# VectorE takes the next group's gathered rows inside the quad it builds before, in a graph kernel with one step per 1024 edges

## The reference, cut to what matters

```python
def _L0_gnn_ref(node_features, edge_index, edge_features, W1, b1, W2, b2, U1, c1, U2, c2):
    src_features = node_features[src]
    msg_input = jnp.concatenate([src_features, edge_features], axis=-1)
    h = jax.nn.relu(msg_input @ W1 + b1)
    messages = h @ W2 + b2
    aggregated = jax.ops.segment_sum(messages, dst, num_segments=N)
    g = jax.nn.relu(jnp.concatenate([node_features, aggregated], axis=-1) @ U1 + c1)
    return g @ U2 + c2
...
h = jnp.maximum(_layernorm(x), 0.0)
x = x + _L0_gnn_ref(h, edge_index, edge_attr_64, ...)
h = jnp.maximum(_layernorm(x), 0.0)
x = x + segment_sum(h[src] * edge_weight[:, None], dst)
```

## Time and profile before

| | |
|---|---|
| median of 3 runs | 3135.02 us (3133.75 to 3136.86) |
| the profiled execution, its own time | 3122.63 us |
| its span | 3120.8 us |
| TensorE busy | 2232.2 us, 72% |
| VectorE busy | 1629.2 us, 52% |
| GpSimd busy | 1560.8 us, 50% |
| ScalarE busy | 849.5 us, 27% |
| mean granted TensorE clock | 0.812 of full |

### The profile page before, as it was taken

One profiled execution on the slowest core, in us unless ns is written; L12 is line 12 of the kernel. 1 busy time (PEld: TensorE's weight loads), 2 busy tenths in 40 slices (PEclk: granted clock), 3 DMA queues, 4 the chain that ended last, 5 costly groups with the idle time before them and its releaser, 6 DMA issues.

```text
span 3120.8 us, 49909 instructions
## 1 busy us (share of the span) xinstructions
PE 2232.2 (72%) x18336; PEld 1691.8 (54%) x18336; DVE 1629.2 (52%) x4964; ACT 849.5 (27%) x1500; POOL 1560.8 (50%) x1635
## 2 busy tenths in 40 slices
PE   4475755666666677677777777777777777777799
PEld 4354544444444455555555555555555655665577
DVE  4445755555555555555554555545555455554455
ACT  4122433222222222222222222223222322222221
POOL 4635255555555545555555455555555544554400
PEclk9867877777777777777777877888888889888899
DMA  4123444433543454355435543553555356525688
GB/s 89 34 91 133 167 135 154 156 129 121 178 137 118 131 186 149 93 167 166 138 108 164 169 132 119 162 170 114 166 166 154 102 160 181 176 78 155 177 275 289
DMA packets 376799, 459.49 MB, mean 147 GB/s; under 512 B 78474, under 2 KB 298890, under 8 KB 372968
## 3 DMA queue, kind: packets, MB, share of 16 engines
q1 hardware_dynamic: 317914, 401.54, 39.4%
q0 software_dynamic: 51712, 53.06, 7.8%
q10 hardware_dynamic: 6926, 1.63, 0.2%
HBM read 281.50 MB, written 174.54 MB: 146 GB/s over the span
## 4 chain that ended last, share of the span: by engine, by line
PE 51%; issue 16%; another core or an unknown queue 15%; DVE 13%; DMA 2%; ACT 1%; SPq 1%; DVEq 0%; ACTq 0%
PE pair L1303 17%; PE pair L1318 9%; PE pair L1342 7%; PE pair L1243 5%; DVE bld L1818 4%; DVE bld L1828 4%; PE pair L1290 3%; PE pair L1349 2%; PE pair L1236 2%; PE pair L1446 1%; DVE rings L1772 1%; PE pair L1376 1%; DMA late_piece<-adjacency 1%; DVE bld L1821 1%
## 5 line engine op out<-in xcount | busy, mean ns | idle before, releaser
L835 POOL DMA_INDIRECT rows<-table,idx x1464 | 1402.6, 958 | 1245.6 <-DVE rings L1772 851.5
L1009 ACT COPY stage<-pair 128x600 f32<-128x600 f32 x808 | 527.8, 666 | 1760.0 <-remote 767.0
L1818 DVE TENSOR_SCALAR bld<-iota_key,key 128x300 bf16<-128x300 f16 x1616 | 536.8, 332 | 798.8 <-remote 509.7
L1303 PE MATMUL pair<-bld 128*128 128x300 bf16 x4848 | 839.1, 328 | 91.8 <-issue 54.1
L1303 PEld LDWEIGHTS pair<-bld 128*128 128x128 bf16 x4848 | 566.1, 122 | 322.3 <-issue 160.4
L1318 PE MATMUL pair<-stage,h 125*64 125x96 f32 x4230 | 380.0, 310 | 191.2 <-issue 188.8
L1828 DVE TENSOR_TENSOR bld<-bld,part 128x512 bf16<-128x512 bf16 x1212 | 490.7, 405 | 0.0
L1318 PEld LDWEIGHTS pair<-stage,h 125*64 125x64 f32 x4230 | 301.6, 179 | 241.5 <-issue 240.8
L1243 PE MATMUL pair<-w1b,rings 128*128 128x128 f32 x1584 | 264.4, 321 | 164.5 <-DVE rings L1772 160.8
L1243 PEld LDWEIGHTS pair<-w1b,rings 128*128 128x128 f32 x1584 | 244.5, 233 | 185.3 <-DVE rings L1772 176.5
L1342 PE MATMUL pair<-late_piece,h 125*64 125x384 f32 (+1 forms) x1040 | 266.5, 642 | 92.9 <-issue 76.8
(11 more groups left out here) (178 smaller groups left out, 1439.1 us busy)
## 6 DMA issues: line engine op xcount, KB each, us to landing
late_piece<-adjacency SPq DMA_DIRECT2D x232, 480.0 KB
rings<-in_edge_attr_dram SPq DMA_DIRECT2D x202, 256.0 KB
adjacency<-stage SPq DMA_DIRECT2D x14, 2160.0 KB
tail<-stage SPq DMA_DIRECT2D x101, 240.0 KB
stage<-tail SPq DMA_DIRECT2D x50, 480.0 KB, 5.9
rows<-table,idx POOLq DMA_INDIRECT x1464
adjacency<-stage SPq DMA_DIRECT2D x10, 1920.0 KB
adjacency<-stage SPq DMA_DIRECT2D x10, 1680.0 KB
```

Source lines behind the costliest of these rows:

```text
L835: pool.indirect_dma_start(out=to[:, t, :], out_offset=None, in_=table, in_offset=bass.IndirectOffsetOnAxis(ap=idx[:, g, t:t + 1], axis=0), ...
L1009: act.copy(tiles[:, g % STAGE, :, 2 * j * WT:2 * (j + 1) * WT].rearrange("p h (o w) -> p o h w", w=WT), build_pair[i % 2][:, :, 0:KEYS].re ...
L1303: last = pe.matmul(build_pair[i // 2 % 2][:, t % 2, 0:KEYS], hot_w[q % 2][k][:, :, u], hot_key[q % 2][:, u, :], start=(k == 0), stop=(k == ...
L1818: return dve.tensor_scalar(hot_key[q % 2][:, u, :], iota_key[:, :], key[:, g, t + u:t + u + 1], None, ALU.is_equal)
```

## The change

For groups 4 and on, `add_fast(s + 1)` is moved from step s + 1 into step s, behind the first key of quad 2s + 2. It gets a wait for the group's edge terms (`q_made`). Groups 0 to 3 stay where they were.

```diff
                 if g >= RAW:
                     gathered_wait(dve, g, g % RING, 0)
-                else:
-                    dve.wait_ge(q_made, g + 1)
+                dve.wait_ge(q_made, g + 1)
                 of = q_bank.rearrange("p (t f) -> p t f", f=D)
...
-            def make_quad(q):
+            def make_quad(q, take=None):
...
                     if k == 0:
+                        if take is not None:
+                            add_fast(take)
                         dve.wait_ge(eq_made, q + 1)
...
                         add_sums(s - 1)
+                    if s < RAW:
+                        add_fast(s)
                     if s < GROUPS:
-                        add_fast(s)
                         make_hot(s)
...
-                            make_quad(q)
+                            make_quad(q, s + 1 if q % 2 == 0 and s + 1 >= RAW else None)
```

## The result

The changed kernel takes 3296.51 us (median of 4 runs, 3288.36 to 3303.15), the kernel before 3134.39 on the same chip (4 runs, 3128.57 to 3136.86). The ratio is 1.0519, 95% interval [1.0491, 1.0547]: 162 us slower, where 100 us less was forecast. The time lies outside the range and on the other side.

A forecast was written before the change was run, and what follows sets the result against it. The bound was taken to be the loop from add through gather burst and release to the next add. Gains of 16 + 62 + 22 = 100 us turn 3122.6 into 3022.6, plus 12.4 for the median: 3035 us, range 2965 to 3180.

The forecast's parts named there:

- the loop: What sets a step with gathers: add, burst 0.96 us later, release about 11.5 later, then VectorE's remaining work before the next add.
- release: Moment when PE's held-up signals reach VectorE and ACT again; taken as fixed, about 11.5 us after the burst of gathers begins.
- two late products: 78 steps: 1.34 us between release and add in place of 2.3; gain 0.8 each, 62 us; steps of 13.9.
- no late product: 97 steps, 79 with gathers: 0 to 0.33 us between release and add for 0.44; gain 0.2 each, 16 us; steps of 12.8.
- It fits, with nothing to spare: PE's late products, tiles 0 to 3 and `make_q` end 12.0 to 13.0 us after the add, against a release at 12.5.
- the stop: Point in a burst from which PE's signals no longer arrive, some 6.5 us after the add; VectorE was to finish its quads before.
- so PE can run them during the burst: Tiles 0 to 3 and `make_q` no longer wait for their own step's add; PE runs them under the gathers, signalled at the release.
- PE becomes the bound: Rival, slower, chance 0.10: PE's chain stretches by 2 us, the 100 steps with late products lose 0.5 each; 3169 us.
- Bursts run together: Rival: POOL's next burst follows without pause, signals stay away; 3242 or 3098 us. Chance 0.14 everywhere, 0.08 in part of the steps.
- PE's wait is the true cost: Rival, faster, chance 0.06: all 160.8 us of PE's edge-term product waiting for the add go; 2974 us.
- The signs named for a wrong forecast: Gathers without pause and steps alternating near 7 and 21 us; or PE idle for microseconds ahead of L1342, L1807 or a load.
- The rule weighed: VectorE and GpSimd exclude each other on a shared port pair; bursts inside a quad up to 2.3 us longer a step; taken as nothing.

The follow-up runs named there:

- e6: Kernel after with the add moved to the step's end, behind both quads and just ahead of the accumulator's add: 3243.10 us, ratio 1.0337 to the kernel before.
- e14: Kernel after with each batch's direct products cut to the first 10 blocks, the others left out: 3062.76 us, ratio 0.9915 to the kernel before.
- e9: Kernel before with only 4 of a group's 8 gathers issued from group 22 on, half the rows left out: 2161.34 us, ratio 0.7001.
- e12: Kernel before with the add in the early place for groups 4 to 104 alone: 3055.89 us against 3084.42, ratio 0.9906.
- e13: Kernel before with each batch's direct products cut to the first 10 blocks, the others left out: 3097.74 us against 3087.66, ratio 1.0027.
- e7: Kernel after with PE's `make_q` put ahead of tiles 0 to 3: 3359.17 us, ratio 1.071 to the kernel before.
- e8: Kernel after with `make_q` one group earlier on PE, ahead of direct and late products: 3366.97 us, ratio 1.0737 to the kernel before.
- e1: Kernel before with the new wait for `q_made` on all groups, the add left in place: 2232.49 us against 2233.34, ratio 1.0002.
- e11: Kernel after, unchanged, repeated on another chip: 3217.90 us against 3084.42 for the kernel before, ratio 1.043.

## Why the prediction was wrong

**Right: the loop.** Add, burst 0.96 later, release some 11.5 later, rest of VectorE's work, add. It held in the kernel after (11.65), in e6 (11.41) and in e14 (11.64), and e9 shows that the gathers make it. e6 gave all steps one length, as the loop says.

**Right in the first half, in part by luck: two late products.** Forecast 13.9, median 13.80. e12, with the change there alone, is 29 us faster. The 28 steps sum to 9.5 us less, 0.34 each where 0.8 was taken. The forecast had only the release set this step. But PE's chain came out equally long, 7.4 + 6.5 = 13.9, and in 23 of the 28 steps the add follows the end of `make_q` within 0.25 us.

**Nearly right in the first half: no late product.** 12.8 was forecast for 13.01; the medians are 12.93 against 13.06, and 12.77 in e14 against 12.92 in e13. That is 0.13 and 0.15, where 0.2 was taken. The 53 steps sum to 4.6 us less, and the 22 behind group 104 to 19.7 more, so the term of 16 us came out as a loss of 15.

**The step that failed is "It fits, with nothing to spare".** The prediction had `late` start "5 to 6 us after the add's start", and from there 7.5 us for late products, tiles 0 to 3 and `make_q`: "13.0 after the add at the most, 12.0 at the least, against a release at 0.96 + 11.5 = 12.5". With two late products behind group 104 the chain took 8.3 + 7.9 = 16.2 us on average, with three 12.4 + 6.1 = 18.5. It went wrong in three ways.

- *`late` starts later.* With two late products it starts 7.4 us after the add (1176.56, 2021.61), not 5 to 6: VectorE is there after 5.0 (1175.94 - 1.88 = 1174.06) and is then held for 1.9. With three it is held to 11.2 us after the add, and the message sum ends 3.8 us after it on PE instead of 2.5 (medians). The prediction let VectorE and its signals through until the stop, and had the stop come behind the accumulator's add.
- *The direct products were left out.* They stand on PE between the message sum and `late`. They were no part of any path before, because there they ran last in the held-up stretch, with nothing waiting. There are 14 in the step at 1169, 30 in that at 2014 and 40 in that at 2664. With 14 they cost nothing: PE was idle for 4.18 us behind them. With 30 they end at 2020.83 + 0.32 = 2021.15, hardly before the accumulator's add, and with 40 they end 13.4 us after the add (median). e13 and e14 show that their length costs the kernel before nothing and decides the kernel after: without most of them 8.3 + 7.9 becomes 7.0 + 6.0.
- *The row runs in the slow part of the burst.* In the step at 2014 four, three and then one matmul of the late products come with gaps of 0.46 to 0.60 us that no wait explains, and PE ends them at 2026.64. In the step with three late products it is the direct products that trickle:

```profile
2663.95 0.69 DVE L1771 TENSOR_TENSOR rings<-rows,pair 128x512 f32<-128x512 f32 x1 [0.66 <-PE pair L1243]
...
2669.17 0.32 PE L1318 MATMUL pair<-stage,h 125*64 125x96 f32 x2 [0.88 <-issue]
2669.92 0.24 PE L1318 MATMUL pair<-stage,h 125*64 125x96 f32 x1 [0.43 <-issue]
...
2670.64 0.39 PE L1318 MATMUL pair<-stage,h 125*64 125x96 f32 x3 [0.47 <-issue]
...
2675.77 0.20 DVE L1805 TENSOR_TENSOR nodes<-nodes,pair 128x40 f32 x1 [6.82 <-remote]
...
2677.06 2.51 PE L1342 MATMUL pair<-late_piece,h 125*64 125x384 f32 x7
...
2681.38 1.05 PE L1243 MATMUL pair<-w1b,rings 128*128 128x128 f32 x8
...
2682.54 0.69 DVE L1771 TENSOR_TENSOR rings<-rows,pair 128x512 f32<-128x512 f32 x1 [0.66 <-PE pair L1243]
```

  From 2669.17 to the release a group of one to four starts every 0.7 or 1.4 us. At the release, 2675.77, VectorE gets only the accumulator's add; late products, tiles and `make_q` all come behind it, and the next add is 6.8 us past the release. The prediction took the stop for something that delays signals, and let PE run on. The words "so PE can run them during the burst" held for the first 3 to 4 us of it in the steps with 30 and 40 direct products (the gaps begin at 2017.96 and 2668.47), and throughout in the step at 1169.

In the two steps shown the chain is 7.5 + 6.0 = 13.5 at 1169, which still passes, and 7.4 + 8.3 = 15.7 at 2014. Over the 49 steps of that kind the loss is 1.8 us each, 87 us; over the 24 with three late products it is 3.4 each, 81 us. Why more direct products make PE's later work slower, beyond their own time, no run shows.

**The rivals.** "PE becomes the bound" was the right one by mechanism (VectorE waits by name for L1349, L1303 and L1243), given 0.10 and 3169 us. Its price was too low: 0.5 us per step with late products, where the second half lost 1.8 with two and 3.4 with three; and it was given no loss without late products, where 22 steps behind group 104 lost 20 us. The direct products run in those too, and with few of them these steps take 13.39 on average (e14), against 15.15. "Bursts run together" did not happen: POOL began each burst after a wait for the add, 181 waits in all. "PE's wait is the true cost" is refuted: that wait went, and the time rose. The signs named for a wrong forecast were PE idle ahead of L1342, which is there (199.0 us of "issue"), and gathers without pause, which are not.

**The rule weighed.** Bursts now begin inside a quad, and a gather has 952 ns on average against 958 before: the burst is not longer, and taking nothing for it was right. The keys are. One that begins while a gather runs takes 432 ns on average, the others 307 (the page's mean over all went from 332 to 355), 38 us of busy time in all, as would fit the rule if it is VectorE that waits. The same page of the Trainium skill ("SBUF — State Buffer", "Who interferes with whom") says "PE and ACT never wait on anyone". Of that port pair it may hold; but PE's gaps while gathers run (442, against 155 with half of the gathers and none on the fast chip) show that the sentence can't be read as leave to put PE's work under a burst without a price.

**Open.** What holds the engines up in a burst (it got smaller with half of the gathers and with a pause, and was absent on one chip; half of the gathers also move half of the rows, so the number of gathers and their traffic aren't told apart), and by what rule PE's gaps come and go (many direct products bring them in the kernel after, but few don't end them in the kernel before). Why e7 and e8 lose more than the kernel after.

## What to carry to other kernels

Before an instruction is moved ahead of work that another engine waits for, write out that engine's whole queue from the signal it is given to the signal it gives back, and take its length from the last steps of the kernel, not only from an early one: a row that grows with the loop and lay under cover can become the path halfway through. When a chain fits "with nothing to spare", each term left out decides the sign; here the early place up to group 104 was a gain of 0.9%, and the change as a whole a loss of 4.3% on the same chip. Where another engine's burst slows a queue, as here, the work beneath it is not free in the later part of the burst; here a pause in the burst was worth more (3.1%) than any move of VectorE's.

## What the runs showed of the hardware

- **The same kernel took 2233 us on one chip and 3084 to 3138 on the others.** On the first the clock granted to TensorE was 0.943 on average (e1), on that of this case 0.812, and VectorE had no long remote waits. One chip's profile is thus no guide to another's bound: 58% of the chain was gathers on the one, while PE led it on the other (51%).
- **Eight gathers in a row hold the engines up, four much less.** On the chips with long remote waits a step of 13.0 us became 7.3 with half of them, more than the 4 x 1.25 = 5 us of issue saved, and VectorE's remote wait at the key fell from 509.7 to 39.1 us.
- **In the held stretch PE moves on in groups of one to four matmuls every 0.7 or 1.4 us** (2669.17, 2669.92, 2670.64), each gap ascribed to "issue". The gap has no releaser in the trace and is easily taken for an idle queue. In the kernel after they nearly go when few direct products stand ahead (28 in e14 against 418 in e11 and 442), though the gathers are the same.
